# Graph attention, 4096 x 256 with a dense bias, on one core: prologue cut into halves, block 1's q moved, last block's sums in the score banks

## What is computed

```python
h = jnp.maximum(_layernorm(x, axis=-1), 0.0)
q = h @ Wq.T + bq
k = h @ Wk.T + bk
v = h @ Wv.T + bv
a = q @ k.T * scale + adj + adj          # scale = 1/sqrt(256)
out = x + softmax(a, axis=-1) @ v
```

## Time and profile before

| | us |
|---|---|
| median of 3 runs | 823.91 (822.46 to 825.2) |
| the profiled execution | 823.64 |
| its span, first to last instruction | 821.80 |
| TensorE busy | 807.6 (98%) |
| VectorE busy | 587.8 (72%) |
| GpSimd busy | 382.8 (47%) |
| ScalarE busy | 361.2 (44%) |

### The profile page before, as it was taken

The page is one execution under the profiler, slowest core; times in us unless marked ns, Lnnn a source line. Parts: engine busy times, 40 slices in busy tenths (PEclk is TensorE's granted clock), DMA queues, the critical chain, the costliest instruction groups (busy, mean ns, idle before and its releaser), DMA issues.

```text
span 821.8 us, 16591 instructions
## 1 busy us (share of the span) xinstructions
PE 807.6 (98%) x6702; PEld 805.4 (98%) x6702; DVE 587.8 (72%) x980; ACT 361.2 (44%) x651; POOL 382.8 (47%) x329
## 2 busy tenths in 40 slices
PE   7899999999999999999999999999999999999998
PEld 6899999999999999999999999999999999999988
DVE  4687777677777777777777777777777777777753
ACT  3684434434443343444334444434444444444364
POOL 2463908263360727346071724618182451818272
PEclk9999999999999999999999999999999999999999
DMA  6350324334332433334243333323333332333200
GB/s 223 114 182 26 104 78 129 91 91 116 91 109 72 130 92 99 106 91 116 67 126 101 93 104 92 115 76 118 103 91 111 90 108 83 111 103 98 84 26 14
DMA packets 43852, 81.68 MB, mean 99 GB/s; under 512 B 4992, under 2 KB 5632, under 8 KB 43776
## 3 DMA queue, kind: packets, MB, share of 16 engines
q1 hardware_dynamic: 43344, 80.10, 33.2%
q10 hardware_dynamic: 432, 0.53, 0.2%
HBM read 76.42 MB, written 4.19 MB: 98 GB/s over the span
## 4 chain that ended last, share of the span: by engine, by line
PE 97%; DVE 1%; ACT 1%; DMA 1%; issue 0%; POOL 0%; ACTq 0%; DVEq 0%
PE ps L309 50%; PE ps L395 15%; PE ps L397 15%; PE ps L396 15%; PE ps L301 1%; DMA w_all<-in_w 1%; PE ps L382 0%; PE ps L375 0%; ACT x_third L460 0%; PE ps L328 0%; PE ps L324 0%; DVE x_res L620 0%; DVE hT L562 0%; POOL v L263 0%; ACT v_full L478 0%
## 5 line engine op out<-in xcount | busy, mean ns | idle before, releaser
L309 PE MATMUL ps<-qhl,hT 128*128 128x256 f32 x3072 | 407.5, 282 | 1.2 <-POOL v L263 1.2
L309 PEld LDWEIGHTS ps<-qhl,hT 128*128 128x128 f32 x3072 | 384.4, 190 | 1.4 <-POOL v L263 1.4
L281 POOL TENSOR_TENSOR ring_a<-ring_a,m_row 128x512 f32<-128x512 f32 x179 | 230.2, 1332 | 215.4 <-ACT m_row L523 215.4
L395 PE MATMUL ps<-v,p_hi 128*128 128x258 f32 x1024 | 291.1, 284 | 1.2 <-DVE x_res L620 1.2
L397 PE MATMUL ps<-v,p_lo 128*128 128x258 f32 x1024 | 288.9, 282 | 0.0
L396 PE MATMUL ps<-v,p_hi 128*128 128x256 f32 x1024 | 288.7, 282 | 0.0
L519 ACT CAST p_hi<-ps 128x512 fp32r<-128x512 f32 x256 | 150.4, 588 | 246.3 <-PE ps L397 244.2
L577 DVE TENSOR_TENSOR ring_a<-ps,ring_a 128x512 f32<-128x512 f32 x179 | 123.4, 689 | 102.3 <-PE ps L309 101.5
L395 PEld LDWEIGHTS ps<-v,p_hi 128*128 128x128 f32 x1024 | 194.0, 189 | 1.4 <-DVE x_res L620 1.4
L397 PEld LDWEIGHTS ps<-v,p_lo 128*128 128x128 f32 x1024 | 194.1, 190 | 0.0
L396 PEld LDWEIGHTS ps<-v,p_hi 128*128 128x128 f32 x1024 | 193.3, 189 | 0.0
(11 more groups left out here) (74 smaller groups left out, 362.9 us busy)
## 6 DMA issues: line engine op xcount, KB each, us to landing
ring_a<-in_adj SPq DMA_DIRECT2D x179, 256.0 KB, 2.7
ring_b<-in_adj SPq DMA_DIRECT2D x77, 256.0 KB, 2.7
x_res<-in_x SPq DMA_DIRECT2D x16, 256.0 KB, 3.0
out<-x_res SPq DMA_DIRECT2D x16, 256.0 KB, 2.0
x_pair<-in_x SPq DMA_DIRECT2D x5, 512.0 KB, 3.8
x_third<-in_x SPq DMA_DIRECT2D x2, 512.0 KB, 3.7
w_all<-in_w ACTq DMA_DIRECT2D x2, 256.0 KB, 3.9
x_pair<-in_x SPq DMA_DIRECT2D x4, 128.0 KB, 4.0
```

The lines of the kernel that those rows point to most:

```text
L281: nc.gpsimd.tensor_tensor(slot_tiles(w), slot_tiles(w), m, ALU.subtract).then_inc(s_sub, 1)
L309: last = nc.tensor.matmul(dst, lhs(a, ib), rhs(c, ib), start=(n == 0), stop=(n == 3 * DB - 1))
L395: nc.tensor.matmul(ps[:, O_BANK + i, 0:VW], hi, v[:, n, 0:VW], start=(n == 0), stop=False)
```

## The change

It has these parts. Numbers of lines are those of the changed kernel where the rows of its order stand.

1. `WARM` is 20 instead of 14.
2. Group 0 of x is handled as two parts of two tiles each (`part_of`), from statistics to h_lo; part p of the later groups is group p - 1. VectorE normalizes part 0 and ScalarE all other parts, group 1 too. SyncE issues tiles 2 and 3 only when tile 0 has landed.
3. The weight product begins when the hi parts exist and takes hi·hi of both output halves first; its halves lie in banks 6 and 7. The bias products follow the first transposes, and bq·bk comes after block 0's q.
4. Block 1's q moves from the start of the prologue to group 3.
5. TensorE waits for the last v_lo before the first sums, no longer before block 1's scores.
6. The last block's sums go to banks 0 and 1 and wait for the last add_adj instead of `finish` of the block before. In each unit the four matmul triples are ordered by query tile first. After the first query tile is complete, its result is finished and stored apart from the second.

```diff
-    WARM = 14
+    WARM = 20
+    Q1_GROUP = 3
+    PARTS = GROUPS + 1
...
+        def part_of(p):
+            if p < 2:
+                return 0, range(p * GT // 2, (p + 1) * GT // 2)
+            return p - 1, range(GT)
+
+        def o_bank(b):
+            return S_BANK if b == BLOCKS - 1 else O_BANK
...
             for j in range(GT):
+                if j == GT // 2:
+                    sp.wait_ge(s_x0[0], 16)
                 sp.dma_start(rows(0)[:, j], x_groups[0, :, j]).then_inc(s_x0[j], 16)
...
-            store(BLOCKS - 1)
-            sp.wait_ge(s_out, 16 * BLOCKS)
+            for i in range(QS):
+                sp.wait_ge((s_last, s_fin)[i], (1, BLOCKS)[i])
+                sp.dma_start(out[BLOCKS - 1, :, i], x_res[:, i]).then_inc(s_out, 16)
+            sp.wait_ge(s_out, 16 * (BLOCKS - 1 + QS))
...
             def multiply_weights():
-                pe.wait_ge(s_nlo, 2)
-                for m in range(DB):
-                    last = split_product(ps[:, V_BANKS[1], m * D:(m + 1) * D],
-                                         lambda a, ob: wqk[:, 0, a, ob, m * P:(m + 1) * P],
-                                         lambda a, ob: wqk[:, 1, a, ob, :])
+                pe.wait_ge(s_nhi, 2)
+                for a, c in ((0, 0), (0, 1), (1, 0)):
+                    if (a, c) == (0, 1):
+                        pe.wait_ge(s_nlo, 2)
+                    for m in range(DB):
+                        for ob in range(DB):
+                            last = nc.tensor.matmul(ps[:, V_BANKS[1] + m, 0:D], wqk[:, 0, a, ob, m * P:(m + 1) * P],
+                                                    wqk[:, 1, c, ob, :], start=(a + c + ob == 0),
+                                                    stop=(a == 1 and ob == DB - 1))
...
             def turn_max(b):
                 pe.wait_ge(s_cols, b + 1)
+                if b == 0:
+                    pe.wait_ge(s_vhi, 2 * GROUPS)
...
             def weigh_values(w):
                 b, u = w // UNITS, w % UNITS
-                if u == 0 and b > 0:
+                if w == 0:
+                    pe.wait_ge(s_vlo, 2 * GROUPS)
+                if u == 0 and b == BLOCKS - 1:
+                    pe.wait_ge(s_add, STEPS)
+                elif u == 0 and b > 0:
                     pe.wait_ge(s_fin, b)
                 pe.wait_ge(s_plo, w + 1)
-                for k in range(KT):
-                    n = KT * u + k
-                    for i in range(QS):
+                for i in range(QS):
+                    for k in range(KT):
+                        n = KT * u + k
...
+                    if w == STEPS - 1 and i == 0:
+                        last.then_inc(s_half, 1)
...
             multiply_weights()
             transpose_h(0)
+            multiply_biases()
             pe.wait_ge(s_glo, 1)
             pe.wait_ge(s_hlo, 1)
             project_q(0)
+            multiply_bias_pair()
+            transpose_h(1)
             pe.wait_ge(s_ulo, 1)
             project_v(0, 0)
-            project_q(1)
-            transpose_h(1)
             scores(0)
-            pe.wait_ge(s_qlo, 2)
+            pe.wait_ge(s_hlo, 2)
+            pe.wait_ge(s_term, 1)
             project_v(0, 1)
+            transpose_h(2)
             scores(1)
             for g in range(1, GROUPS):
                 if g + 1 < GROUPS:
-                    transpose_h(g + 1)
-                pe.wait_ge(s_hlo, g + 1)
+                    transpose_h(g + 2)
+                pe.wait_ge(s_hlo, g + 2)
                 project_v(g, 0)
                 scores(2 * g)
-                project_v(g, 1)
-                scores(2 * g + 1)
-            pe.wait_ge(s_vlo, 2 * GROUPS)
+                if g == Q1_GROUP:
+                    pe.wait_ge(s_vhi, 2 * g)
+                    project_q(1)
+                    scores(2 * g + 1)
+                    pe.wait_ge(s_qlo, 2)
+                    project_v(g, 1)
+                else:
+                    project_v(g, 1)
+                    scores(2 * g + 1)
...
+            act.wait_ge(s_g, 1)
+            nc.scalar.mul(G[:, 0], ps[:, V_BANKS[1]:V_BANKS[1] + DB, 0:D], QSCALE).then_inc(s_ghi, 1)
+            h_hi(0)
             act.wait_ge(s_wv, 16)
             nc.scalar.copy(wv_T[:, 0, :, 0:D], wv_nat).then_inc(s_whi, 1)
...
             act.wait_ge(s_uhi, 1)
+            normalize(1)
             q_hi(0)
+            act.wait_ge(s_bqk, 1)
+            nc.scalar.mul(term_bias[:, :], ps[:, V_BANKS[1], 0:1], QSCALE).then_inc(s_term, 1)
+            h_hi(1)
+            normalize(2)
             act.wait_ge(s_wlo, 1)
+            act.wait_ge(s_term, 1)
             v_hi(0, 0)
-            q_hi(1)
-            h_hi(1)
+            h_hi(2)
             v_hi(0, 1)
-            normalize(2, range(GT)).then_inc(s_norm, 1)
+            normalize(3)
...
+            def finish_last():
+                dve.wait_ge(s_xb, BLOCKS)
+                for i in range(QS):
+                    dve.wait_ge((s_half, s_pv)[i], (1, STEPS)[i])
+                    at = o_bank(BLOCKS - 1) + i
+                    nc.vector.reciprocal(inv_sum[:, i:i + 1], ps[:, at, D:D + 1]).then_inc(s_inv, 1)
+                    dve.wait_ge(s_inv, BLOCKS + i)
+                    nc.vector.scalar_tensor_tensor(x_res[:, i], ps[:, at, 0:D], inv_sum[:, i:i + 1], x_res[:, i],
+                                                   ALU.mult, ALU.add).then_inc((s_last, s_fin)[i], 1)
```

More of the change, by code:

```diff
@@ L291, in _, with transpose_h @@
                 nc.tensor.transpose(ps[:, X_BANK, 0:P], ident[:, :], ident[:, :])
[L293 to L296, removed]
+            def transpose_h(p):
+                g, tiles = part_of(p)
+                if p == 0:
+                    pe.wait_ge(s_norm0, 1)
+                else:
+                    pe.wait_ge(s_norm, p)
+                    pe.wait_ge(s_hlo, p)
                 for ib in range(DB):
-                    if g > 0:
-                        pe.wait_ge(s_hlo, g)
-                    for j in range(GT):
+                    for j in tiles:
                         last = nc.tensor.transpose(ps[:, HT_BANK + ib, j * P:(j + 1) * P],
@@ L330, in multiply_weights, with multiply_bias_pair @@
                                          bq_col[:, ob:ob + 1], start=(ob == 0), stop=(ob == DB - 1))
+                for m in range(DB):
+                    for ob in range(DB):
+                        last = nc.tensor.matmul(ps[:, V_BANKS[0], 2 * m:2 * m + 2],
+                                                wqk_nat[:, 0, ob, m * P:(m + 1) * P],
+                                                bk_pair[:, ob, :], start=(ob == 0), stop=(ob == DB - 1))
+                last.then_inc(s_bmm, 1)
+            def multiply_bias_pair():
+                pe.wait_ge(s_bb, 1)
+                pe.wait_ge(s_const, 1)
                 for ob in range(DB):
-                    last = nc.tensor.matmul(ps[:, V_BANKS[0], 3 * DB:3 * DB + 1], ones[:, :],
+                    last = nc.tensor.matmul(ps[:, V_BANKS[1], 0:1], ones[:, :],
                                             bias_products[:, ob:ob + 1], start=(ob == 0), stop=(ob == DB - 1))
-                last.then_inc(s_bmm, 1)
+                last.then_inc(s_bqk, 1)
             def project_q(b):
-                if b == 1:
-                    pe.wait_ge(s_qlo, 1)
                 if b >= 2:
@@ L629, in _ @@
                                         ALU.subtract).then_inc(s_nlo, 1)
+            dve.wait_ge(s_rstd, 1)
+            for j in range(GT // 2):
+                last = nc.vector.tensor_scalar(rows(0)[:, j], rows(0)[:, j], mean_var[:, 0, j, 0:1],
+                                               rstd[:, 0, j:j + 1], ALU.subtract, ALU.mult)
+            last.then_inc(s_norm0, 1)
             for j in range(GT // 2, GT):
                 tile_stats(0, j)
-            group_stats(0)
+            part_stats(1)
+            dve.wait_ge(s_ghi, 1)
+            nc.vector.scalar_tensor_tensor(G[:, 1], ps[:, V_BANKS[1]:V_BANKS[1] + DB, 0:D], QSCALE,
+                                           G[:, 0].bitcast(f32), ALU.mult, ALU.subtract).then_inc(s_glo, 1)
+            h_lo(0)
             dve.wait_ge(s_bc, 16)
@@ L668, in _ @@
                 if g + XB < GROUPS:
-                    group_stats(g + XB)
+                    part_stats(g + XB + 1)
+                if g == Q1_GROUP:
+                    q_lo(1)
                 add_adj(2 * g)
@@ L675, in _ @@
                 b, u = s // UNITS, s % UNITS
-                if s not in HOLD and due(s) > 0 and due(s) % UNITS == 0:
+                if s not in HOLD and 0 < due(s) < STEPS and due(s) % UNITS == 0:
                     finish(due(s) // UNITS - 1)
@@ L687, in _ @@
                     q_lo(b + 1)
+            finish_last()
 def kernel(**inputs):
```

150 lines of the change are left out of this document (71 added, 79 removed).

## The result

| | before | changed |
|---|---|---|
| median of 9 runs each | 822.52 (820.79 to 825.2) | 820.15 (818.69 to 820.37) |
| profiled execution | 823.64 | 820.26 |
| its span | 821.8 | 818.5 |

The ratio of the times is 0.9962, with a 95% interval from 0.9947 to 0.9978, so the changed kernel is faster. By how much depends on what is compared: the medians lie 2.4 us apart, which is just under the 0.3% (2.5 us) that the prediction asked for, the means 3.1 and the two profiled executions 3.4. The runs of the changed kernel stand in two groups, three from 818.69 to 819.09 and six from 819.85 to 820.37. The profiled one is of the second.

A forecast was written before the change was run, and what follows sets the result against it. TensorE, busy 98% of the span, was taken to bound the kernel. Gains of 3.7 (prologue), 0.6 (v_lo wait), 0.9 (last block's sums) and 0.8 (tail) made 6.0: 823.64 - 6.0 = 817.6 us, range 815.6 to 822.3.

The forecast's parts named there:

- A: Prologue, likeliest case, 50%: TensorE's clock is at 2.4 GHz by 7 to 8 us and stays there; 817.6 us.
- Rival D: Prologue, 13%: early rise, but the idle 2.8 before group 2's transposes lets the clock fall, losing 1.7 to 3.3; 819.3 to 820.9.
- C: Prologue, rival, 13%: the clock rises while the bias products run, q starts at 13.2; 820.2 us.
- Clock in the prologue: Prologue: unbroken TensorE work brings 2.4 GHz by 7 to 8 us, so q starts at 10.6 instead of 17.65.
- B: Prologue, rival, 20%: warm-up and transposes raise nothing, the clock stays low through block 0's q; 821.4 us.
- Up to group 2's transposes: Prologue: q's lo half done at 14.1, then a chain of 11.05; transposes start at 25.15 instead of 31.18, 6.0 earlier.
- Block 1's q in group 3: Group 3 of the prologue: moved q costs 1.43 of matmuls there and a 0.9 wait for its lo half.
- Wait for v_lo: Before block 1's scores: moving the wait removes 1.2, but 0.6 returns as a wait for max_rows; gain 0.6.
- Last block's sums: Last block: sums in banks 0 and 1 remove a wait of 1.2, 0.3 returns for p_lo; gain 0.9.
- The order inside a unit costs nothing: Units of sums: four runs of three accumulations become two of six, at no cost.
- Tail: After the last matmul: one x_res instruction instead of two and a store of 128 KB instead of 256; gain 0.8.

The follow-up runs named there:

- The filled kernel: The changed kernel with 24 further matmuls of 256 columns in TensorE's idle time before group 2's transposes; 818.58 us, ratio to before 0.9942.

## Why the prediction was right or wrong

The forecast of the direction and the range were right: 820.15 lies between 815.6 and 822.3, below the 821.4 that I took for faster. The likeliest case, A with 817.6, was not what came: the gain was 3.4 between the profiled executions, not 6.0. Rival D was, with 13%: its 819.3 to 820.9 holds the median and the profiled 820.26. The time alone would have fitted C (820.2) as well; the traces decide, since the rise came in the warm-ups and the fall behind the idle stretch. Part of the fit is luck: all these times are counted from 823.64, and the median of nine runs of before is 1.1 lower. Counted from there D gives 818.2 to 819.8, which 820.15 just misses.

- *Clock in the prologue*: right in what it gives. The rise came at 5.0, sooner than the 7 to 8 that I took, the spacing was 0.12 from 6.03 on but for two waits for the lo parts, and q started at 10.44 (10.6 forecast). The rule that I had weighed against it, that transposes don't count for the clock (the Trainium skill, "TensorE: Matmul & The Clock Gate", Part 4), does not hold here: the 20 transposes took 4.10 instead of 4.5, so the rise came while they ran. It did so in six of the eleven profiles with 20 or 25 of them; in the other five it came in the weight product behind them. B, which rested on the rule, fell.
- *Up to group 2's transposes*: right, by the chain that was named (q's lo half done at 14.1, ScalarE's normalizations from 17.80 on): 25.21 for 25.15, behind ScalarE and with an idle stretch of 2.77 (2.8 forecast).
- The step that failed is A's that this idle stretch leaves the clock alone. It cost 1.57 in the profile; D had put it at 1.7 to 3.3. The filled kernel, which kept the clock and those 1.57, shows cause and size. I had seen 1.85 at the high clock and 2.77 is half as long again; that should have weighed more than 13%.
- *Block 1's q in group 3*: right in kind, too small in size: 2.66 for 2.33. The wait behind q was 0.57 by starts (45.26 + 1.43 to 47.26) for 0.9, but two later groups were late by 0.55 in all, behind the v pair that q pushed back, which the sum did not have.
- *Wait for v_lo*: 0.66 for 0.6, and 0.77 in the kernel that puts it back.
- *Last block's sums*: 0.70 for 0.9, and 0.83 in the kernel that undoes it; the wait of 0.3 for p_lo came.
- *The order inside a unit costs nothing*: wrong, 0.45 in the profile and up to 0.8 by the kernel that undoes it. q's twelve matmuls at 22.45 could not show an effect of about a quarter of a ns in each.
- *Tail*: 0.70 for 0.8.

Sum of the steps in the profile: 5.97 - 1.57 - 2.66 + 0.66 - 0.45 + 0.70 + 0.70 = 3.35, against a difference of 3.38 of the profiled executions. The medians differ by 2.4 only, since the profiled execution of before is 1.1 slower than its median.

## What to carry to other kernels

When a change opens idle time on the engine that bounds the kernel, look for work to put there before asking anything else: here the change had moved 12 matmuls out of a prologue that then idled for 4.5 us, and moving them back won 4.4 us. Follow the chain that ends the idle time to the first engine that waits while it could do later work: moving two rows of VectorE's list was worth 2.5. And where a change reorders an inner loop, take its pace from whole blocks: 0.04 us in a block of 48 us made 0.6 us here.

## What the runs showed of the hardware

- Transposes on TensorE brought the clock up. Of the 11 profiles with 20 or 25 of them, their spacing went from 213 to 109 ns with nothing else run so far in six, between 4.2 and 5.1. In the other five it rose in the weight product behind them, between 6.5 and 7.6, once after 25 transposes that all ran at the low level.
- Idleness of 2.77 us at the high clock was followed by 3.4 us at 1.2 GHz in both profiles that have it (from 25.5 with 20 warm-ups, from 27.3 with 14). By the mean granted clock, 0.998 against 0.999 and 1.0, it was so in six of the nine runs of the changed kernel. With the stretch filled by useless matmuls, or cut by block 1's q into waits of 0.8 and 0.3, it did not happen; 1.85 of idleness in the kernel before did nothing.
- Three profiles lost the clock again soon after an early rise. It fell at 11.1, 11.2 and 11.7 in the three profiles with a rise at 4.2, 4.4 and 4.9, and not there in those with a rise at 4.7, 5.0 and 5.1 or later. In the first two TensorE had idled 0.6 and 0.9 behind the warm-ups and then worked on without a gap of that size, from 8.5 or 8.9 on for 1.7 us on bias products of 1 and 2 columns. In the third it had idled 1.2 and 1.0. What brings this fall no run isolates.
- Two runs of six matmuls into a bank in each unit, rather than four of three, cost 0.035 to 0.05 us in each block of 16 units (13 blocks in 620.5 instead of 619.9 to 620.1).
